# Last one-head attention and last mixture of a four-level network: products of weights and the first four tiles of rows made in the stage in front

## The chip, the cores and the metric

The kernel runs on one core of a Trainium2 chip: one program that computes the whole network in one launch. The metric is the device time of that launch in microseconds; three runs of the kernel before gave 1704.18, 1707.31 and 1710.19, median 1707.31 us.

## The reference

x has 32 batches of 32 tokens with 256 features (1024 tokens), context 32 x 257 x 192. Four levels follow each other, each with cross attention, self attention and a feed-forward part, and each part is `x = x + part(layernorm(x), ...)`. What matters here is the end of it:

```python
def L3_attn(x, Wq, bq, Wk, bk, Wv, bv, Wo, bo):        # one head, within each batch
    q, k, v = x @ Wq.T + bq, x @ Wk.T + bk, x @ Wv.T + bv
    qk = einsum('bsd,btd->bst', q, k)
    theta = 0.5 + 0.2 * sigmoid(qk) + 0.15 * tanh(qk) + 0.1 * relu(qk)
    out = einsum('bst,btd->bsd', softmax(theta), v)
    return out @ Wo.T + bo

def L3_ffn(x, Wg, bg, W1, b1, W2, b2):                  # mixture of 8 experts, best 2 of each token
    gates = softmax(x @ Wg + bg)
    g = gates on the two largest, divided by their sum
    return sum over e of g[e] * (gelu(x @ W1[e] + b1[e]) @ W2[e] + b2[e])

x = x + L2_ffn(layernorm(x), ...)                       # mixture with a capacity for each expert
x = x + L3_xattn(layernorm(x), ctx_768, ...)            # cross attention with the context
x = x + L3_attn(layernorm(x), ...)
x = x + L3_ffn(layernorm(x), ...)
```

## The kernel before

x lies in SBUF as 8 tiles of 128 tokens (four batches to a tile) by 256 features, beside xn (the normalised rows) and xnT (the same transposed, 2 chunks of 128 features by 1024 tokens). Each part of the network is a stage, a function of its own with one block in which the five engines have a list each; the lists are written out by hand, and semaphores order them against each other. At the end of a block all engines meet at a barrier, so a stage starts when the last of them is through, SP (which issues the DMAs) included.

The stages around the change, in order: `stage_scan`, `stage_moe_capacity` ("moecap" in tile names), `stage_xattn3` ("xattn"), `stage_attn3` (which calls `stage_one_head`, "attn"), `stage_moe` ("moe").

A stage that starts with a layernorm makes it in one of two ways. `Norm` (line 107) does all 8 tiles in the stage: statistics and moments on VectorE (L153, L156), the power -0.5 on GpSimd (L183, L186), rows on VectorE (L166), for attn3 some of them on ScalarE (L211), transposes on TensorE (L201), copies into xnT on ScalarE (L221), with `warm` (L61) giving TensorE idle matmuls to do during the statistics. `Ahead` splits it: rows 0 to 3 (tiles 0 to 3) are made in the end of the stage in front, rows 4 to 7 at the start of the own stage, beside matmuls on the first half. Its parts are `statistics`, `moments`, `power`, `rows`, `turn` and `take`, and its tiles and semaphores belong to the core. Six stages have it, among them the one-head attention of level 1 (`stage_attn1`), which shares the function `stage_one_head` with attn3; the branches `soft_theta` are attn3's.

**attn3 before.** SP issues eight loads of its weights and biases (L2098 to L2103), then `ew.sp`: two clearings of spare rows (L2994, L2995) and 16 loads of 1 MB, W1 and W2 of the eight experts of the last mixture (L3328, L3329, tile moe_w). The SBUF of these 16 MB is given out when `stage_xattn3` has ended, so they can't be loaded sooner. TensorE waits for its own eight loads, makes Wq.Wk ("QK", L2131), transposes xn, folds the biases (`fold_biases`, L2140 to L2148), makes Wv.Wo ("VO", L2131), then queries times QK (L2168), scores (L2182), values (L2193) and probabilities times values (L2201). VectorE adds each result to x (L2295).

**The mixture before.** `Norm` for all tiles, then `TopTwo`: logits by 32 matmuls (L2925) behind one wait for all four of its loads (L2908 to L2911, issued at the front of the stage by SP), choice of two experts on VectorE, ranks, then lists of rows for 23 blocks. Rows and gates are stored to DRAM (L3006 to L3009), GpSimd gathers each block's rows (L3415), TensorE does the two layers of each block (L3466, L3476), GpSimd adds the results into the output in DRAM. TensorE and VectorE wait for all of moe_w before the first block.

**The end of xattn3 before.** A pipeline over steps s = 0 to 12: scores(s), turned probabilities (s-1), probabilities times context (s-2, L3808), turned output (s-3, L3819), and for pairs of tiles values (L3830) and projection (L3840). In the last steps only the later pieces are left.

Of the kernel before, what the change touches and what calls it, by code (L numbers as in the profile page):

```python
# [6 lines left out]
ALU = mybir.AluOpType  # L7
ACT = mybir.ActivationFunctionType
F32 = mybir.dt.float32
# [6 lines left out]
P = 128  # L16
# [89 lines left out]
class Norm:  # L106
# [31 lines left out]
    def all_ready(self, eng, end=TILES):  # L138

        eng.wait_ge(self.xn_ready, len([t for t in self.by_dve if t < end]))  # L140
        if self.by_act:
            eng.wait_ge(self.xn_act_ready, len([t for t in self.by_act if t < end]))

# [1898 lines left out]
def stage_one_head(core, name, wq, wk, wv, wo, b_qkv, bo, ew=None, hw=None, ln=None, nx=None, lw=None):  # L2042
    nc, d = core.nc, core.dram
    soft_theta = hw is None
    with ExitStack() as ctx:
        st = Stage(core, ctx, name)
        if soft_theta:
            ln = Norm(st, shared=True)
            wq_s, wk_s, wv_s = [st.sb(n, [P, CD, D]) for n in ("wq", "wk", "wv")]
            qk = st.sb("qk", [P, CD, D])  # L2050
        else:
            wq_s, wk_s, wv_s, qk = hw.wq, hw.wk, hw.wv, hw.qk
        tT = st.sb("tT", [P, CD, TOKENS])
        v = core.xn if soft_theta else st.sb("v", [P, TILES, D])
# [6 lines left out]
        loaded = st.sem("loaded")  # L2061
        qk_done, qk_ready = st.sem("qk_done"), st.sem("qk_ready")
# [10 lines left out]
        if soft_theta:  # L2073
            wo_s, bo_s, b_s = st.sb("wo", [P, CD, D]), st.sb("bo", [P, D]), st.sb("b", [P, 3 * CD])
            bq_wide, bv_wide = st.sb("bq_wide", [P, CD, P]), st.sb("bv_wide", [P, CD, P])
            vo, key_b, query_b = st.sb("vo", [P, CD, D]), st.sb("key_b", [P, CD]), st.sb("query_b", [P, CD, SEQ])
            both_b, half_b, out_b = st.sb("both_b", [P, 1]), st.sb("half_b", [P, 1]), st.sb("out_b", [P, D])
            th_half, th_full = st.sb("th_half", [P, TILES * SEQ]), st.sb("th_full", [P, TILES * SEQ])
            relu, theta = st.sb("relu", [P, TILES * SEQ]), st.sb("theta", [P, TILES * SEQ])
            wide_ready, folded, fold_ready = st.sem("wide_ready"), st.sem("folded"), st.sem("fold_ready")  # L2080
            vo_done, vo_ready, out_b_ready = st.sem("vo_done"), st.sem("vo_ready"), st.sem("out_b_ready")
            relu_ready, tanh_ready, bo_added = st.sem("relu_ready"), st.sem("tanh_ready"), st.sem("bo_added")
            LOADS = 8
        else:
            vo = wv_s
# [3 lines left out]
        QK, VO, FOLD, OUT = bank[4], bank[5], bank[6][:, 0:2 * CD + 1], bank[6][:, D:2 * D]  # L2089
# [5 lines left out]
        def _(sp):  # L2095
            if soft_theta:
                for to, m in [(wq_s, wq), (wk_s, wk)]:
                    sp.dma_start(to[:, :, :], m.rearrange("(c p) n -> p c n", p=P)).then_inc(loaded, 16)  # L2098
                for n in range(3):
# [2036 lines left out]
```

## Time and profile before

| | before |
|---|---|
| median of 3 runs | 1707.31 us (1704.18 to 1710.19) |
| the profiled execution, its own time | 1711.28 us |
| its span | 1709.4 us |
| mean granted TensorE clock | 0.961 |
| TensorE busy | 1535.2 us, 90% of the span |
| VectorE, ScalarE, GpSimd busy | 1059.1, 837.4, 765.8 us |
| bytes moved by DMA | 204.51 MB, mean 120 GB/s |

Times in the profile are microseconds from the start of the span unless marked ns. PE is TensorE's matmuls, PEld its weight loads, DVE VectorE, ACT ScalarE, POOL GpSimd, SP the engine that issues most DMAs; SPq and POOLq are their queues' own instructions. `out<-in` names the tiles that an instruction writes and reads, `xN` counts instructions, and a bracket gives the engine's idle time in front and what ended it. In a timeline row the first number is the start, the second the time from there to the end of the last instruction of the row. PEclk 1.00 means 2.4 GHz and 0.50 means 1.2 GHz.

### The profile page before, as it was taken

The numbers are of one execution on the slowest core, as the hardware profiler recorded it, in microseconds if no ns is written. First come the engines' busy times: TensorE is split into PE (matmuls) and PEld (weight loads), VectorE is DVE, ScalarE is ACT, GpSimd is POOL, SyncE is SP. The second block draws the span as 40 slices with busy tenths as digits, with TensorE's granted clock in tenths as the row PEclk, the third lists the DMA queues.
The fourth block names the chain that finished last, engine by engine and source line by source line (L and its number), as shares of the span: only waits on it lengthen the run. The fifth ranks groups of instructions, "written<-read, shape, count | busy, mean of one in ns | idle before, by whom it ended". The sixth has DMA issues, their size and how long they took to land. (4 is left out here: it accounts for less than half of the span.)

```text
span 1709.4 us, 37142 instructions
## 1 busy us (share of the span) xinstructions
PE 1535.2 (90%) x13507; PEld 1315.5 (77%) x13507; DVE 1059.1 (62%) x2934; ACT 837.4 (49%) x2414; POOL 765.8 (45%) x894
## 2 busy tenths in 40 slices
PE   7999999988788999987999999998859788859998
PEld 6898898957567999975888988874539744649997
DVE  4888877645866888865866776748941132353332
ACT  4666666645335888851766666650013222213332
POOL 7666555442338999953311111226833311213332
PEclk9999999999999999999999999999979988879999
DMA  8554454312003333312633333425047272952221
GB/s 267 185 164 157 161 172 158 105 68 83 1 1 116 132 131 131 133 42 83 196 116 106 106 106 113 145 78 181 1 124 216 27 232 93 345 178 33 38 39 26
DMA packets 127221, 204.51 MB, mean 120 GB/s; under 512 B 21034, under 2 KB 92362, under 8 KB 126658
## 3 DMA queue, kind: packets, MB, share of 16 engines
q1 hardware_dynamic: 119016, 188.83, 34.2%
q0 software_dynamic: 6720, 8.79, 3.3%
q10 hardware_dynamic: 1306, 4.51, 0.8%
q8 instruction: 111, 1.82, 0.4%
q14 instruction: 68, 0.56, 0.1%
HBM read 161.76 MB, written 41.14 MB: 119 GB/s over the span
## 5 line engine op out<-in xcount | busy, mean ns | idle before, releaser
L1073 DVE TENSOR_SCALAR xattn_oT<-banks,xattn_last 128x256 f32<-128x256 f32 x254 | 110.9, 478 | 90.5 <-PE banks L854 90.1
L962 ACT ACTIVATE xattn_probs<-banks,xattn_negmax 128x257 f32<-128x257 f32 x256 | 123.9, 484 | 62.4 <-DVE xattn_negmax L1054 62.3
L967 ACT ACTIVATE xattn_probs<-xattn_probs,xattn_rsum 128x257 f32<-128x257 f32 x256 | 131.8, 515 | 1.4 <-DVE xattn_rsum L1058 1.4
L1350 POOL TENSOR_SCALAR xattn_probs<-xattn_probs,xattn_rsum 128x257 f32<-128x257 f32 x128 | 119.5, 934 | 23.2 <-DVE xattn_rsum L1622 23.1
L1054 DVE TENSOR_REDUCE xattn_negmax<-banks 128x1 f32<-128x257 f32 x256 | 106.4, 416 | 34.7 <-PE banks L820 33.1
L765 POOL COPY ctx_stat<-xattn_mv 128x2 f32<-128x2 f32 x32 | 6.0, 187 | 237.1 <-DVE xattn_mv L1087 237.1
L973 ACT CAST xattn_probsT_hi<-banks 128x256 fp32r<-128x256 f32 x256 | 95.5, 373 | 31.5 <-PE banks L829 27.6
L1063 DVE TENSOR_TENSOR xattn_probsT_lo<-banks,xattn_probsT_hi 128x256 fp32r<-128x256 f32 x256 | 105.0, 410 | 7.1 <-ACT xattn_probsT_hi L973 6.0
L829 PE MATMUL banks<-ident,xattn_probs 128*128 128x128 f32 x512 | 103.9, 285 | 3.6 <-ACT xattn_probs L967 3.2
L715 POOL TENSOR_SCALAR xattn_ctxT<-xattn_rawT 128x514 fp32r<-128x514 f32 x32 | 49.8, 1558 | 100.0 <-issue 94.7
L816 PE MATMUL banks<-xattn_ctxT,xattn_qk_hi 128*128 128x258 f32 x256 | 93.7, 366 | 0.5 <-DVE xattn_qk L1050 0.5
L3466 PE MATMUL banks<-moe_xinT,moe_w_now 128*128 128x128 f32 x736 | 88.3, 279 | 0.0
L3466 PEld LDWEIGHTS banks<-moe_xinT,moe_w_now 128*128 128x128 f32 x736 | 86.5, 196 | 0.1
L849 PE MATMUL banks<-xattn_probsT_hi,xattn_ctxN 128*128 128x256 f32 x256 | 85.0, 332 | 1.1 <-issue 1.1
L3424 POOL DMA_INDIRECT out_dram<-moe_y_slots,moe_row_u x23 | 36.4, 1584 | 110.2 <-DVE moe_y_slots L3591 107.2
L798 PE MATMUL banks<-xattn_qT,xattn_wk 64*128 64x128 f32 x1024 | 73.3, 283 | 11.9 <-DVE xattn_qT L1039 10.2
L3476 PE MATMUL banks<-moe_w,moe_hT 128*128 x368 | 83.1, 379 | 0.0
L2727 POOL TENSOR_TENSOR scan_product<-scan_state,scan_qT 128x1024 f32<-128x1024 f32 x32 | 70.0, 2187 | 20.5 <-DVE scan_state L2874 18.4
L798 PEld LDWEIGHTS banks<-xattn_qT,xattn_wk 64*128 64x128 f32 x1024 | 62.2, 187 | 20.9 <-issue 13.1
L3510 ACT ACTIVATE moe_hT<-banks,moe_b_now 128x128 f32<-128x128 f32 x184 | 52.6, 368 | 47.1 <-PE banks L3466 47.1
L871 PE MATMUL banks<-xattn_oT,xattn_wv 128*64 128x128 f32 x1024 | 69.1, 278 | 7.2 <-issue 6.0
L780 PE MATMUL banks<-xnT,xattn_wq 128*128 128x128 f32 x512 | 69.7, 283 | 6.1 <-ACT xnT L221 2.3
(516 smaller groups left out, 5087.1 us busy)
## 6 DMA issues: line engine op xcount, KB each, us to landing
xattn_ctxT<-ctx_partsT SPq DMA_DIRECT2D x64, 516.0 KB, 4.0
xattn_ctxN<-ctx_partsN SPq DMA_DIRECT2D x64, 384.0 KB, 4.1
ctx_partsT<-xattn_ctxT SPq DMA_DIRECT2D x32, 516.0 KB, 2.7
moe_w<-in_L_ffn_W SPq DMA_DIRECT2D x16, 1024.0 KB, 12.9
ctx_partsN<-xattn_ctxN SPq DMA_DIRECT2D x32, 384.0 KB, 3.6
moecap_w_early<-in_L_ffn_w SPq DMA_DIRECT2D x10, 1024.0 KB, 9.2
xattn_rawN<-in_ctx SPq DMA_DIRECT2D x32, 192.0 KB, 2.7
xattn_raw<-in_ctx SPq DMA_DIRECT2D x32, 192.0 KB, 5.1
```

The costliest lines, as they stand in the source:

```text
L798: mm = nc.tensor.matmul(bank[:, k * P:(k + 1) * P], wk_s[r, h // 2, g % 2 * P:(g % 2 + 1) * P], qT[r, h // 2, :], start=True, stop=True, t ...
L816: nc.tensor.matmul(out, unit(qk1[0]), part(0, 0), start=True, stop=False)
L829: mm = nc.tensor.transpose(TB[n % 2][:, c * P:(c + 1) * P], probs[:, n % RING, c * P:(c + 1) * P], core.ident[:, :])
L849: nc.tensor.matmul(front[:, 0:2 * P], first_hi(c), hi[:, c], start=(c == 0), stop=False)
L962: nc.scalar.activation(probs[:, n % RING, :], SB[n % 2][:, 0:KV], ACT.Exp, bias=negmax[:, n % RING:n % RING + 1], accum_out=psum[:, n % RI ...
L967: nc.scalar.mul(probs[:, n % RING, :], probs[:, n % RING, :], rsum[:, n % RING:n % RING + 1]).then_inc(norm_ready, 1)
L973: nc.scalar.copy(probsT[0][:, n // 2 % PAIRS, :, n % 2, :], TB[n % 2][:, 0:2 * P].rearrange("p (c n) -> p c n", c=2)).then_inc(probsT_hi_r ...
L1054: nc.vector.tensor_reduce(negmax[:, n % RING:n % RING + 1], SB[n % 2][:, 0:KV], AX.X, ALU.max, negate=True).then_inc(negmax_ready, 1)
L1063: nc.vector.tensor_tensor(lo, TB[n % 2][:, 0:2 * P].rearrange("p (c n) -> p c n", c=2), hi, ALU.subtract).then_inc(probsT_ready, 1)
L1073: nc.vector.tensor_scalar(oT[k][:, heads, b, :], by_head(out_banks(n)[k][:, k * 2 * P:(k + 1) * 2 * P]), last[:, k, j * PER_TILE + b:j * P ...
L1350: nc.gpsimd.tensor_scalar(probs[:, n % RING, :], probs[:, n % RING, :], rsum[:, n % RING:n % RING + 1], None, ALU.mult).then_inc(norm_read ...
L3466: mm = nc.tensor.matmul(H[n % 2][k][:, f * P:(f + 1) * P], w1_now[:, c, at:at + P], xinT[:, n % 2, c, :], start=(c == 0), stop=(c == CD - 1))
```

## The change

Four things are moved. (1) The weights and biases of attn3 get tiles of their own at the other end of SBUF (`SoftWeights`), loaded by SP in `stage_moe_capacity` behind the last expert's weights. (2) Their products and the folding of the biases are made in the last steps of `stage_xattn3`: folding at s = 8, QK at s = 9, VO at s = 10, in banks that are free by then; ScalarE and VectorE take them a step later; GpSimd widens two bias columns at the start of that stage. (3) attn3's layernorm becomes an `Ahead`: statistics of rows 0 to 3 on VectorE at s = 9, rows at s = 12, transposes on TensorE at s = 11, copies at the end. (4) The last mixture's layernorm becomes an `Ahead` too: rows 0 to 3 in the end of attn3, rows 4 to 7 in the mixture, whose TensorE list is now: gate matmuls of half 0, transposes of rows 4 to 7, gate matmuls of half 1. The idle matmuls of `warm` fall away in both stages. SP's list in attn3 holds only `ew.sp`. attn3's values go into a tile of their own instead of xn, since xn now holds the next stage's rows.

```diff
+class SoftWeights:
+    LOADS = 8
...
+    def sp(self, sp):
+        for to, m in zip((self.wq, self.wk, self.wv, self.wo), self.drams):
+            sp.dma_start(to[:, :, :], m.rearrange("(c p) n -> p c n", p=P)).then_inc(self.loaded, 16)
+        for n in range(3):
+            sp.dma_start(self.b[:, n * CD:(n + 1) * CD], self.b_drams[n]).then_inc(self.loaded, 16)
+        sp.dma_start(self.bo[:, :], self.bo_dram.partition_broadcast(P)).then_inc(self.loaded, 16)
...
+    def product(self, out, left, right):
+        for c in range(CD):
+            for k in range(CD):
+                mm = self.nc.tensor.matmul(out[:, c * D:(c + 1) * D], left[:, k, c * P:(c + 1) * P], right[:, k, :],
+                                           start=(k == 0), stop=(k == CD - 1))
+        return mm
...
@@ stage_one_head @@
         @block.sync
         def _(sp):
             if soft_theta:
-                for to, m in [(wq_s, wq), (wk_s, wk)]:
-                    sp.dma_start(to[:, :, :], m.rearrange("(c p) n -> p c n", p=P)).then_inc(loaded, 16)
...
                 ew.sp(sp)
...
-            if soft_theta:
-                ln.warm(pe, 7)
-                pe.wait_ge(loaded, 16 * LOADS)
-                product(QK, wq_s, wk_s).then_inc(qk_done, 1)
-                ln.pe(pe)
-                fold_biases()
-                product(VO, wv_s, wo_s).then_inc(vo_done, 1)
-                pe.wait_ge(qk_ready, 1)
+            pe.wait_ge(hw.qk_ready, 1)
             for n in range(2):
-                if soft_theta:
-                    pe.wait_ge(ln.xnT_ready, CD * (n + 1))
-                else:
-                    if n:
-                        ln.turn(pe, 1, LATE)
-                    ln.transposed(pe, n)
+                if n:
+                    ln.turn(pe, 1, LATE)
+                ln.transposed(pe, n)
...
-            if not soft_theta:
-                nx.turn(pe, 0, NEXT)
+            nx.turn(pe, 0, NEXT)
...
@@ stage_moe_capacity, SP @@
                 cw.load(sp, e)
+            hw.sp(sp)
             bring(sp, range(0, TILES, 2))
...
@@ stage_moe @@
         @block.tensor
         def _(pe):
-            ln.warm(pe, 7)
-            ln.pe(pe)
             for h in range(2):
-                pe.wait_ge(ln.xnT_ready, CD * (h + 1))
+                ln.transposed(pe, h)
                 gate.pe(pe, h)
+                if h == 0:
+                    ln.turn(pe, 1, LATE)
...
@@ stage_xattn3 @@
+    FOLD_AT, QUERIES_KEYS_AT, VALUES_OUT_AT, TURN_NEXT_AT = TILES, TILES + 1, TILES + 2, TILES + 3
...
+        FOLD, QUERIES_KEYS, VALUES_OUT, NEXT = SB[0], SB[1], TB, OB
...
+            hw.wide(pool)
...
+            nx.power(pool, 0)
...
+                if s == FOLD_AT:
+                    pe.wait_ge(scaled_ready, TILES - 1)
+                    hw.fold_biases(pe, FOLD)
+                elif s == QUERIES_KEYS_AT:
+                    pe.wait_ge(scaled_ready, TILES)
+                    hw.queries_keys(pe, QUERIES_KEYS)
+                elif s == VALUES_OUT_AT:
+                    pe.wait_ge(probsT_ready, 2 * TILES)
+                    hw.values_out(pe, VALUES_OUT)
+                elif s == TURN_NEXT_AT:
+                    pe.wait_ge(o_ready, TILES)
+                    nx.turn(pe, 0, NEXT)
...
+                if s == QUERIES_KEYS_AT + 1:
+                    hw.take_queries_keys(act, QUERIES_KEYS)
+                elif s == VALUES_OUT_AT + 1:
+                    hw.take_values_out(act, VALUES_OUT)
+            nx.take(act, 0, NEXT)
...
+                if s == TURN_NEXT_AT + 1:
+                    nx.rows(dve, 0)
...
+                if s == FOLD_AT + 1:
+                    hw.take_biases(dve, FOLD)
+                    dve.wait_ge(x_done, 2)
+                    for t in Norm.HALVES[0]:
+                        nx.statistics(dve, t)
+                    nx.moments(dve, 0)
```

## Rows read from the trace of the kernel before

**Rows 1.** The chain that ended last, in order of time: start, us, what.

```profile
1508.26 1.52 PE banks L201 x8
...
1509.78 3.49 PE banks L2925 x32
```

**Rows 2.** Timeline of SP's issues, attn3 to mixture.

```profile
1452.85 0.39 SPq L2098 DMA_DIRECT2D attn_wq<-in_L_attn_Wq  x1
...
1457.95 0.59 SPq L3328 DMA_DIRECT2D moe_w<-in_L_ffn_W  x1
...
1495.13 0.95 SPq L3329 DMA_DIRECT2D moe_w<-in_L_ffn_W  x1
1502.92 0.37 SPq L2908 DMA_DIRECT2D moe_gate_w<-in_L_ffn_Wg  x1
```

**Rows 3.** Busy times by stretch; last PEclk, DMA share, GB/s.

```profile
1435.40:1448.20 12.80, 9.82 (x77) 5.38 (x76) 2.03 (x6) 4.30 (x10) 0.00 (x0) 1.00 0.01 1
1448.20:1452.80 4.60, 3.64 (x8) 2.36 (x8) 0.69 (x1) 0.00 (x0) 0.00 (x0) 0.63 0.00 0
...
1473.00:1502.90 29.90, 25.35 (x321) 17.76 (x320) 11.46 (x24) 4.71 (x12) 4.04 (x6) 0.94 1.06 376
```

**Rows 4.** DMA issues, KB each, us to landing (single issues, in six stretches).

```profile
moe_w<-in_L_ffn_W SPq DMA_DIRECT2D x1, 1024.0 KB, 7.0
...
moe_w<-in_L_ffn_W SPq DMA_DIRECT2D x1, 1024.0 KB, 12.2
...
moe_gate_up_to<-in_up_to SPq DMA_DIRECT2D x1, 128.0 KB, 3.7
...
moe_gate_w<-in_L_ffn_Wg SPq DMA_DIRECT2D x1, 8.0 KB, 2.9
...
moecap_gate_w<-in_L_ffn_gate_w SPq DMA_DIRECT2D x1, 8.0 KB, 1.9
...
moecap_w_early<-in_L_ffn_w SPq DMA_DIRECT2D x2, 1024.0 KB, 6.2
```

**Rows 5.** Waits of SP in attn3: total, times, longest, in us.

```profile
SPq L2045 <- PEq L2045: 6.6, 1, 6.6
```

**Rows 6.** Timeline of TensorE in the end of xattn3.

```profile
1437.76 0.33 PE L3819 MATMUL banks<-ident,xattn_o_norm 128*128 128x128 f32 x1 [1.03 <-ACT xattn_o_norm L3897]
...
1443.07 1.89 PE L3840 MATMUL banks<-xattn_wo,xattn_aT 128*128 128x256 f32 x8
...
1448.21 3.64 PE L3840 MATMUL banks<-xattn_wo,xattn_aT 128*128 128x256 f32 x8 [0.93 <-ACT xattn_aT L3914]
```

**Rows 7.** Timeline of TensorE in attn3: a product, and a part of the folding.

```profile
1460.56 3.78 PE L2131 MATMUL banks<-attn_wk,attn_wq 128*128 128x256 f32 x8 [3.82 <-DMA attn_bo<-in_L_attn_bo]
...
1466.53 0.95 PE L2140 MATMUL banks<-attn_b,attn_wk 128*128 128x1 f32 x8
```

**Rows 8.** Timeline of SP's issues in the capacity mixture.

```profile
1306.62 0.51 SPq L3042 DMA_DIRECT2D moecap_w_early<-in_L_ffn_w  x1
1366.35 1.77 SPq L3099 DMA_DIRECT2D x<-moecap_sum  x4
```

**Rows 9.** Timeline of the level-1 one-head attention.

```profile
767.40 3.70 PE L2168 MATMUL banks<-xnT,attn_qk 128*128 128x512 f32 x8 [1.16 <-ACT xnT L276]
...
780.74 1.03 PE L2201 MATMUL banks<-attn_v,attn_probsT 128*128 128x256 f32 x4
...
791.09 0.38 SPq L451 DMA_DIRECT2D xattn_wq<-in_L_xattn_w_q  x1
```

**Rows 10.** Timeline of attn3: first scores, first probabilities times values.

```profile
1480.00 0.31 PE L2182 MATMUL banks<-xnT,attn_tT 128*32 128x32 f32 x4
...
1496.97 1.03 PE L2201 MATMUL banks<-xn,attn_probsT 128*128 128x256 f32 x4
```

**Rows 11.** Timeline of the mixture: first layer of blocks 0 and 1.

```profile
1532.28 6.05 PE L3466 MATMUL banks<-moe_xinT,moe_w_now 128*128 128x128 f32 x32
...
1538.39 3.74 PE L3466 MATMUL banks<-moe_xinT,moe_w_now 128*128 128x128 f32 x32
```

More of the change, by code:

```diff
@@ L2107, in _ @@
         def _(pool):
+            ln.power(pool, 1)
+            nc.gpsimd.memset(probsT[:, :, :], 0.0).then_inc(probsT_zero, 1)
+            ln.normalised(pool, 1)
             if soft_theta:
[L2109 to L2114 removed]
@@ L2123, in _ @@
                 nc.gpsimd.tensor_tensor(x_plus[:, :, :], core.x[:, :, :], core.xn[:, :, :], ALU.add).then_inc(x_plus_ready, 1)
-                nx.power(pool, 0)
+            nx.power(pool, 0)
         @block.tensor
         def _(pe):
-            def product(out, left, right):
-                for c in range(CD):
-                    for k in range(CD):
-                        mm = nc.tensor.matmul(out[:, c * D:(c + 1) * D], left[:, k, c * P:(c + 1) * P], right[:, k, :],
-                                              start=(k == 0), stop=(k == CD - 1))
-                return mm
@@ L2185, in _ @@
             if soft_theta:
-                pe.wait_ge(vo_ready, 1)
+                pe.wait_ge(hw.vo_ready, 1)
             else:
@@ L2296, in _ @@
                                                ALU.mult, ALU.add).then_inc(x_done, 1)
-                if t == 4 and not soft_theta:
+                if t == 4:
                     dve.wait_ge(x_done, 4)
@@ L2301, in _ @@
                     nx.moments(dve, 0)
-            if not soft_theta:
-                nx.rows(dve, 0)
+            nx.rows(dve, 0)
 def head_weights(core, ctx, outer):
@@ L3003, in store @@
         for h, half in enumerate(Norm.HALVES):
-            ln.all_ready(sp, half[-1] + 1)
+            ln.normalised(sp, h)
             rows = self.x[half[0] * P:(half[-1] + 1) * P, 0:D]
@@ L3404, in _ @@
         def _(pool):
-            ln.pool(pool)
+            ln.power(pool, 1)
             gate.pool(pool)
@@ L3492, in _ @@
         def _(act):
-            ln.act(act)
+            ln.take(act, 1, LATE)
             gate.act(act)
@@ L3520, in _ @@
         def _(dve):
-            ln.dve(dve)
+            for t in Norm.HALVES[1]:
+                ln.statistics(dve, t)
+            ln.moments(dve, 1)
+            ln.rows(dve, 1)
             step = Chain(dve, steps)
@@ L3743, in _ @@
                 moments(t)
+            nx.power(pool, 0)
         @block.tensor
```

182 lines of the change are left out of this document (89 added, 93 removed).

## The prediction

> **What bounds the kernel now.** I read the page first: TensorE is busy nearly everywhere, but the slices around the two last stages thin out. The chain of work that ended last [rows 1] reaches back only to the start of the last mixture: statistics of all eight tiles, VectorE's and GpSimd's part, transposes, then 32 gate matmuls ending at 1513.27. In front of it the chain stops at a stage barrier, so I cut the end of the span at the barriers by SP's first issue of each stage [rows 2]: last one-head attention ("attn3") from 1452.85, mixture from 1502.92. That makes 50.1 us for attn3, and 60.4 us from attn3's start to the end of the gate. Call attn3's start S before and S' after the change; everything behind the gate is common to both kernels, so the sum is: how much later is S', and how much less than 60.4 us lies between S' and the end of the gate.
>
> The view that decides is not a compute engine's. SP issues 16 loads of the experts' weights (moe_w, 1 MB each, 16.8 MB) inside attn3, because their SBUF is only free then. The DMA engines run them at 376 GB/s through the whole rest of the stage [rows 3]. The first is issued at 1457.95 and lands 7.0 us later, at 1464.95 (S+12.1); the last is issued at 1495.13 and lands 12.2 us later, at 1507.33 (S+54.5) [rows 2, 4]: 15 further MB in 42.4 us. SP is held in its issues by the full queue and is done at 1496.1; it then waits 6.6 us for the barrier at the end of attn3 [rows 5]. So two limits lie close behind the compute path: the stage can't end before SP has issued its last load, and the gate's own loads stand behind 16.8 MB on the same queue.
>
> **The change part by part.**
>
> *End of the cross attention ("xattn3"), price of the moved work on TensorE.* Now TensorE has three waits of about 1 us there: 1.03 us before each of the last two turns of the normalised output, 0.93 us before the last projection [rows 6]. Added: 20 one-column matmuls and 4 of 256 columns (bias folding), two products of 8 matmuls each, 8 transposes. Eight one-column matmuls take 0.95 us with the last one's tail, so 20 take about 2.2 [rows 7]; 8 matmuls of 256 columns take 1.89 at the full clock [rows 6], so 4 take 0.94 and a product 1.9; 8 transposes took 1.52 with short waits for their rows in it [rows 1], so 1.0 to 1.5. Folding 3.1 less the 1.03 wait that it covers is +2.1; queries-keys 1.9 - 1.03 = +0.9; values-out, in front of nothing that waits, +1.9; transposes 1.0 to 1.5 against 0.93 = +0.1 to +0.6. Together +5.1. The last projection now runs at the low clock, 3.64 us for 8 matmuls against 1.89, just after a wait [rows 3, 6]; with the waits filled it may stay at 2.4 GHz, which gives 1.75 back: +3.4. Were all added work at 1.2 GHz it would cost about double (a product took 3.78 us at that level [rows 7]): +11. I take +4.0, between the two near cases. VectorE's share (five bias copies, statistics, moments and rows of four tiles) falls in its waits for TensorE, which does 8 to 10 us of work between two things that it wants of VectorE; in its order the copies stand behind the sums that ScalarE needs. ScalarE's four copies stand behind what the chain needs of it, the last two beside the projection. GpSimd's two widenings come in a stage start where it waits for loads anyway; its power stands behind its last moments of the context. I price these at 0; their cover is TensorE's added work itself, and if VectorE were late with the rows TensorE would wait in front of its last projection, at most 2 us.
>
> *Loads moved on SP's queue.* The eight small loads (1.2 MB) go from the front of attn3 to the capacity mixture behind the last expert's load, after which SP issues nothing from 1307.1 to 1366.35, when it brings x back [rows 8]: eight issues and 3 us of transfers fit there, 0. In attn3 the first moe_w issue moves from S+5.1 to about S'+1.2, with only the two clearings ahead of it. Two 1 MB loads issued into an empty queue landed 6.2 us after issue in the middle [rows 4], so about 5 for the first and 7.5 for the second; the first lands at S'+6.5 to 8.5, I take 7.3 (S+12.1 before), and at the same 42.4 us for the rest the last lands at S'+49.7, 4.8 us sooner in the stage.
>
> *attn3's compute.* Products, biases and rows 0 to 3 leave the stage. Scores start now at 1480.00, that is S+27.2 [rows 10]. The one-head attention of level 1 already has the new form: its second block of queries starts at 767.40, 6.8 us into its stage (from 760.6), and takes 3.7, so scores could begin at S'+10.5 [rows 9]. From scores to the product with the probabilities attn3 takes 16.97 us (1480.00 to 1496.97 [rows 10]), and from there to the next stage the level-1 attention, which prepares rows 0 to 3 for its follower, takes 10.35 (780.74 to 791.09 [rows 9]). Sum 37.8 us instead of 50.1. SP's limit: the last issue stays 12.2 us before the last landing, so S'+37.5, done 0.9 later: S'+38.4. The two meet; attn3 shrinks by about 11.7 us, and the mixture begins near S'+38.4.
>
> *The mixture.* Preparing rows 0 to 3 earlier would let the gate start sooner by a few us, but its four loads are now issued 11 us before the stream of moe_w has landed. They used to be issued behind a nearly drained queue and landed in 2.9 (weights) to 3.7 us (the triangular constant, at 1508.0) [rows 4]; one matmul wait covers all four. Now they land with the stream's end or a little after it: S'+50.0, from 49 to 52. TensorE, idle since about S'+37, then does 16 gate matmuls, 8 transposes of rows 4 to 7 (which stand behind these in its order, so are held by the loads too), waits for ScalarE's copies, and does 16 more. After an idle of similar length the first 32 weight-bound matmuls of the experts take 6.05 us against 3.74 for the next 32 [rows 11], so I take the first gate half at the low level: 3.5 (double of half of 3.49 [rows 1]), 1.5 for the turn, 1.4 for the copies, 1.8 to 3.5 for the second half: 8.2 to 9.9, take 9.1; all at the full clock it would be 1.75 + 1.1 + 1.4 + 1.75 = 6.0. End of the gate: S'+59.1 against S+60.4: -1.3. The 18 us of VectorE and GpSimd work behind it don't change; stores of the rows land by about S'+60, and the gathers that need them come near S'+73.
> The Trainium skill, "TensorE: Matmul & The Clock Gate", section "What's actually happening", says that the throttled state is the default and activity lifts it. The trace agrees: the low level stands in 1448.2 to 1452.8 behind a wait and 1.00 in the busy stretch before [rows 3]. By the rule the gate costs 9.1; without it, 6.0, and the end would come 3.1 sooner.
>
> **The sum.** +4.0 - 1.3 = +2.7 us. Against the profiled execution (1711.3 us, span 1709.4) that is 1714.0; the median of the runs is 1707.3, 4.0 lower, and the prediction stands against it: **1710.0**. The 12 us taken from attn3 are mostly lost again: before the change the experts' load and the compute ended within a few us of each other, and only the compute is shortened. Bounds of the unknown costs: tail +3.4 to +11, stream end S'+49 to 52, gate 6.0 to 9.9. All three at their low end: 3.4 + (55.0 - 60.4) = -2.0; a bad case, half of the added work at the low level: 8 + (61.9 - 60.4) = +9.5.
>
> **The rivals.**
> *The gate's loads pass the stream* (the faster side). For: the gate's weights, issued at 1502.92, landed at 1505.8, 1.5 us before the last moe_w that was issued 7.8 us earlier [rows 2, 4]. Against: the same load took 1.9 us in the capacity mixture, where the queue was empty, so it did wait 1.0 us here. Price if they pass freely: the mixture starts at S'+38.4 and the loads land 5.1 us into it as now, the gate ends 11.5 us into it, S'+49.9; -10.5 + 4.0 = -6.5, so 1700.8. Chance 0.08.
> By the Trainium skill, "DMA: Bandwidth & Descriptors", section "Queues, rings and completion order", descriptors of one ring are taken up in order on each DMA engine though a later one may complete its write first. By that rule passing is limited to small amounts like the 1.5 us seen, and the rival dies; the trace agrees as far as it goes.
> *The tail of xattn3 at 1.2 GHz* (slower side). The clock there is uneven: 1.00 until 1448.2, then 0.63 [rows 3], though TensorE was mostly busy. If it falls as soon as the folding starts, the added work costs +11 and the other matmuls up to 2 us more: +13 - 1.3 = +11, 1718. It decides from about 2 us of added cost over my +4.0: then the total passes +5.1, a measurable loss. Chance, with milder forms, 0.24.
> *The clock holds and the stream starts promptly:* -2 to +1 us, 1705 to 1708, chance 0.25; it is the lower half of my case.
> *The move doesn't shorten attn3 at all*, because SP's issues stretch: then M moves, but the gate still hangs on the stream; no different time. It is inside the forecast.
>
> **How the numbers follow.** Forecast case (+1 to +5 us) 0.40, the clean case 0.25, passing loads 0.08, something of that sign that I don't see 0.03, slow tail 0.24. A measurement of this kernel tells about 0.3% (5.1 us) from no change. Faster by more: 0.11; within: 0.65; slower: 0.24. Range: from -6 (part of the passing case, and the spread of 3 us that the runs show) to +10: 1701.5 to 1717.5.
>
> **What would show it.** Right: attn3 about 38 us long with SP issuing until just before its end; the last moe_w landing near S'+50; TensorE waiting for a DMA of the gate's loads for 5 us or more in the mixture; xattn3's last stretch about 4 us longer, its three waits gone. Wrong: gate matmuls that start within 7 us of the mixture's start (passing loads), a granted clock of 0.5 through the tail of xattn3, or an attn3 that is longer than 45 us, which would put the statistics of rows 4 to 7 in front of the gate again.

## The result: 0.29% slower, and the profile after

The changed kernel takes 1716.06 us, median of 20 runs (1709.96 to 1722.84), against 1709.93 us (1703.97 to 1720.87, 20 runs) for the kernel before on the same chip: a ratio of 1.0029, 95% interval 1.0015 to 1.0043. In this kernel's time that is +5.0 us (+2.6 to +7.4); forecast were +2.7. (The ratio is not the quotient of the two medians, which would be 1.0036, or 6.1 us, inside the same interval.)

The profiled execution of after took 1713.57 us (span 1711.7, mean clock 0.958) against 1711.28 (1709.4, 0.961), a difference of only 2.3. That number hides something: xattn3 starts 4.3 us sooner in it (SP's first load of the context at 1367.63, before at 1371.97), in front of everything that bears on the time here; over all kernels below that start lies between 1367.6 and 1377.2. So I cut the end of each span at four points that all these kernels share: SP's first issue in xattn3, in attn3 and in the mixture, and GpSimd's first gather of rows. All lengths below are differences of two starts in the timelines of SP and GpSimd; the clock is TensorE's granted clock in the ten microseconds from 50 to 60 us into xattn3, "held" where it stayed at 1.00 in them and "fell" where it didn't; it says nothing of the rest of the stage.

| kernel | xattn3 | clock there | attn3 | mixture to first gather | attn3's start to first gather | rest of the span |
|---|---|---|---|---|---|---|
| before | 80.9 | 0.50 fell | 50.1 | 24.6 | 74.7 | 181.9 |
| after | 87.2 | 0.61 fell | 39.1 | 36.2 | 75.2 | 181.6 |
| e1 turn first | 84.5 | 0.64 fell | 38.9 | 33.0 | 71.8 | 181.8 |
| e2 gate's loads first | 80.0 | 1.00 held | 39.6 | 26.4 | 66.0 | 181.7 |
| e3 two experts late | 84.4 | 0.61 fell | 35.7 | 29.3 | 65.0 | 182.1 |
| e4 before, gate's loads first | 82.7 | 0.50 fell | 46.0 | 25.7 | 71.7 | 180.5 |
| e5 light tail | 78.7 | 0.61 fell | 39.7 | 36.0 | 75.7 | 181.0 |
| e6 norm left in the mixture | 84.2 | 0.61 fell | 39.1 | 33.0 | 72.0 | 181.9 |
| e7 idle matmuls in the gate's wait | 80.3 | 1.00 held | 39.2 | 33.4 | 72.7 | 181.8 |
| e8 = e2 + e5 | 83.7 | 0.63 fell | 41.2 | 26.3 | 67.5 | 180.9 |
| e9 before, filled | 77.6 | 1.00 held | 50.2 | 24.6 | 74.8 | 181.7 |
| e10 after, filled | 80.8 | 1.00 held | 39.9 | 36.0 | 76.0 | 181.4 |
| e11 = e2 + e3 + e5 | 78.8 | 0.61 fell | 39.0 | 27.1 | 66.1 | 181.9 |
| e12 = e11, filled | 77.7 | 1.00 held | 41.9 | 27.2 | 69.2 | 180.8 |

The last column is nearly constant, so what happens behind the first gather is common to all, as the prediction assumed. The first two rows hold the result. The 11.0 us that attn3 lost came back as 11.6 in the mixture, and xattn3 grew by 6.3. The chain that ended last used to start with the statistics of the mixture and lead through the transposes to the gate [rows 1]. In after it goes through SP and a load (start, us, what):

```profile
1493.88 3.82 SPq L2911
...
1499.48 6.08 DMA moe_gate_up_to<-in_up_to
...
1505.70 3.56 PE banks L2928 x16
1509.26 1.81 PE banks L272 x8
...
1511.10 1.08 ACT xnT L279 x2
...
1512.22 3.60 PE banks L2928 x16
```

SP's issues in after, the counterpart of [rows 2]: the first expert's load 1.2 us into attn3 (5.1 before), the last one until 1493.49, and then the gate's four loads. The issue of an 8 KB load alone holds SP for 3.82 us, where it held it for 0.37 before.

```profile
1454.82 0.53 SPq L2997 DMA_DIRECT2D moe_rows<-in_zeros  x1
1455.40 0.59 SPq L2998 DMA_DIRECT2D out_dram<-in_zeros  x1
1456.04 0.59 SPq L3332 DMA_DIRECT2D moe_w<-in_L_ffn_W  x1
...
1492.55 0.94 SPq L3333 DMA_DIRECT2D moe_w<-in_L_ffn_W  x1
1493.88 3.82 SPq L2911 DMA_DIRECT2D moe_gate_w<-in_L_ffn_Wg  x1
...
1499.48 0.43 SPq L2914 DMA_DIRECT2D moe_gate_up_to<-in_up_to  x1
```

What these loads took from issue to landing (KB, then us; four single issues in four stretches), the counterpart of [rows 4]: 9.6 us for the gate's weights and 6.1 for the triangular constant, where it was 2.9 and 3.7.

```profile
moe_w<-in_L_ffn_W SPq DMA_DIRECT2D x1, 1024.0 KB, 5.3
...
moe_w<-in_L_ffn_W SPq DMA_DIRECT2D x1, 1024.0 KB, 12.2
...
moe_gate_w<-in_L_ffn_Wg SPq DMA_DIRECT2D x1, 8.0 KB, 9.6
...
moe_gate_up_to<-in_up_to SPq DMA_DIRECT2D x1, 128.0 KB, 6.1
```

TensorE in the mixture of after, and its clock in the two stretches (in the second fence the columns are as in [rows 3]). It does nothing for 16.94 us, the last 11.8 of them in the mixture, waiting for the constant, and then runs all of the gate at 1.2 GHz.

```profile
1505.70 3.56 PE L2928 MATMUL banks<-moe_gate_w,xnT 128*128 128x8 f32 x16 [16.94 <-DMA moe_gate_up_to<-in_up_to]
1509.11 1.95 PE L272 MATMUL banks<-ident,xn 128*128 128x128 f32 x8
1512.22 3.58 PE L2928 MATMUL banks<-moe_gate_w,xnT 128*128 128x8 f32 x16 [1.16 <-ACT xnT L279]
```

```profile
1493.80:1505.60 11.80, 0.00 (x0) 0.00 (x0) 3.06 (x12) 0.00 (x0) 1.27 (x2) 0.50 1.03 314
1505.60:1516.00 10.40, 8.94 (x40) 8.47 (x40) 0.06 (x1) 1.07 (x2) 0.60 (x2) 0.50 0.96 294
```

The end of xattn3 in after, the counterpart of [rows 6]: the three waits are gone, the moved work stands in their place, and the last projection takes 1.99 us, not 3.64.

```profile
1436.45 1.65 PE L2102 MATMUL banks<-attn_wo,attn_bv_wide 128*128 128x256 f32 x4
...
1442.92 1.99 PE L2079 MATMUL banks<-attn_wk,attn_wq 128*128 128x256 f32 x8
...
1446.69 1.89 PE L2079 MATMUL banks<-attn_wo,attn_wv 128*128 128x256 f32 x8
...
1450.83 1.09 PE L272 MATMUL banks<-ident,xn 128*128 128x128 f32 x8
1451.83 1.99 PE L3850 MATMUL banks<-xattn_wo,xattn_aT 128*128 128x256 f32 x8
```

### The profile page after: what moved, and what is told of

Its sections match the earlier page's. It is cut to its first block and busy times, and to the rows that moved or that the text cites. A ratio compares the mean times of both kernels' runs of the same rounds, so it can differ in the third digit from the quotient of the medians.

```text
span 1711.7 us, 37082 instructions
## 1 busy us (share of the span) xinstructions
PE 1526.9 (89%) x13475; PEld 1310.2 (77%) x13475; DVE 1060.8 (62%) x2936; ACT 835.3 (49%) x2410; POOL 766.8 (45%) x894
## 5 line engine op out<-in xcount | busy, mean ns | idle before, releaser
L718 POOL TENSOR_SCALAR xattn_ctxT<-xattn_rawT 128x514 fp32r<-128x514 f32 x32 | 49.9, 1559 | 97.4 <-issue 92.4
L2730 POOL TENSOR_TENSOR scan_product<-scan_state,scan_qT 128x1024 f32<-128x1024 f32 x32 | 70.0, 2186 | 22.3 <-DVE scan_state L2877 20.4
L2877 DVE TENSOR_TENSOR_SCAN scan_state<-banks,scan_decay 128x528 f32<-128x528 f32 x64 | 75.0, 1241 | 1.5 <-PE banks L2759 1.5
L874 PE MATMUL banks<-xattn_oT,xattn_wv 128*64 128x128 f32 x1024 | 69.2, 278 | 7.2 <-issue 6.1
```

## The experiments

Theory: attn3 is now bound by SP's issue of the experts' loads, the gate by loads that stand behind them, and the work moved into xattn3 is paid there in full. The rival explanations for the loss are the tail of xattn3 alone (its price or its clock), and the split gate. Each ratio below is against the kernel before on the same chip (29 to 35 runs), with 12 runs of the edited kernel, 7 in e3 and 6 in e8.

### e2: the gate's loads ahead of the experts'

The four loads get tiles and a semaphore of their own and are issued in attn3 in front of `ew.sp`; `gate.sp` in the mixture falls away.

```diff
+        gl = GateLoads(core, ctx, ew.E, dram["L3_ffn_Wg"], dram["L3_ffn_bg"])
...
+                gl.sp(sp)
                 ew.sp(sp)
...
-            gate.sp(sp)
```

> The changed kernel with the gate's four loads issued by SP in attn3 in front of the experts' 16 loads, into tiles of their own. Theory: the mixture starts about 40 us after attn3's start and the gate ends 9 to 10 us into it, at 50 instead of 61: 11 us less, about 0.9965 of the kernel before; the other constants (b2, 1 MB) then land about when VectorE wants them, which can cost 0 to 2 us of this. Rival (the stream of 16.8 MB also bounds what comes behind the gate, through the stores of the rows): 0 to 3 us less. Rival (loads are not the bound): no change, 1.003.

Measured: 0.9971 (0.9957 to 0.9985). From attn3's start to the first gather it takes 66.0 us, 9.2 less than after. The first gate half starts 0.2 us after the mixture does:

```profile
1493.09 3.55 PE L2949 MATMUL banks<-early_gate_w,xnT 128*128 128x8 f32 x16 [5.61 <-PEq L2126]
1496.62 1.97 PE L272 MATMUL banks<-ident,xn 128*128 128x128 f32 x8
1499.76 3.58 PE L2949 MATMUL banks<-early_gate_w,xnT 128*128 128x8 f32 x16 [1.16 <-ACT xnT L279]
```

So the loads were what the gate waited for, and four small issues in another place turn the loss into a gain of 0.3%, somewhat less than expected. What is late next is the barrier: attn3 still takes 39.6 us (5.61 us of it TensorE's wait for the stage's end).

### e4: the same early loads in the kernel before

The same edit on the kernel before.

> The kernel before with the same early gate loads as in the run of that kind on the changed kernel. Theory (before the change the layernorm's chain reached the gate at 1509.6, 1.5 us after the last of its loads had landed, so the loads only became the bound by the change): no difference, 1.000, within 1 us. Rival (the loads or the stream already set the gate's time before): 1 to 5 us less.

Measured: 0.9986 (0.9968 to 1.0004), no difference that can be told. There the gate starts when its transposes and TensorE's earlier work are done, not when a load lands (it then takes 4.81 us and not 3.49, since the granted clock falls to 0.50 in its second half):

```profile
1506.48 1.41 PE L201 MATMUL banks<-ident,xn 128*128 128x128 f32 x8 [0.20 <-DVE xn L166]
1508.20 1.41 PE L201 MATMUL banks<-ident,xn 128*128 128x128 f32 x8 [0.32 <-DVE xn L166]
1509.44 4.81 PE L2946 MATMUL banks<-early_gate_w,xnT 128*128 128x8 f32 x32
```

The edit is worth about 10 us to the changed kernel (0.9971 against 1.0029 is 0.58%) and 0.14% or nothing to the one before: the exposure of these loads was made by the change. (In this run attn3 took 46.0 us, 4.1 less than in before, at a clock of 1.00 in its second twelve microseconds instead of 0.83; the ratio shows no gain of that size, so I take it for a difference of this one execution.)

### e3: two experts' loads left to the mixture

Experts 6 and 7 (four of the sixteen loads) are issued in the mixture behind its small loads.

```diff
-        for e in range(self.E):
+        for e in range(first, end):
...
+            ew.sp(sp, 6, E)
             rows.store(sp, ln, gate, stored, begun)
```

> The changed kernel with the loads of experts 6 and 7 (4 MB of 16) issued in the mixture, behind the gate's loads and constants, instead of in attn3. Theory (SP's held issues set the end of attn3, the stream the gate's start): attn3 ends with its compute, about 35.5 us after its start instead of 39; the gate's loads find 12 MB nearly landed and land at about 40, the gate ends at about 50 instead of 61: 11 us less, 0.9965 of the kernel before. Rival: the later end of the stream (about 54) or the stores behind it hold the first block, and 0 to 3 us are left.

Measured: 0.9958 (0.9941 to 0.9975). Attn3 takes 35.7 us instead of 39.1; it is then ended by arithmetic, and SP has been idle for 9 us (its last issue in attn3 ends 26.6 us into it):

```profile
1483.78 0.47 SPq L3334 DMA_DIRECT2D moe_w<-in_L_ffn_W  x1
1493.36 0.37 SPq L2911 DMA_DIRECT2D moe_gate_w<-in_L_ffn_Wg  x1
...
1499.69 3.25 SPq L3333 DMA_DIRECT2D moe_w<-in_L_ffn_W  x1
1502.98 1.12 SPq L3334 DMA_DIRECT2D moe_w<-in_L_ffn_W  x1
1504.14 6.30 SPq L3009 DMA_DIRECT2D moe_rows<-xn  x2
```

This shows the other limit: SP's issues end attn3 in after, 3.3 us behind where arithmetic ends it here. The cost is in the last line: the stores of the rows are now the ones that are held, and the first gather waits for the store of the gates behind them (`<-DMA moe_rows<-moe_gate_weight`), not for the list of rows.

### e1: all transposes ahead of the gate

```diff
+            ln.turn(pe, 1, LATE)
             for h in range(2):
                 ln.transposed(pe, h)
                 gate.pe(pe, h)
-                if h == 0:
-                    ln.turn(pe, 1, LATE)
```

> The changed kernel with one swap in the mixture's TensorE list: transposes of rows 4 to 7 in front of the first gate half instead of behind it. Theory (the gate waits for its own loads, which stand behind the stream of expert weights): in the changed kernel the wait ends 50.9 us after attn3's start and gate, transposes, copies and gate take 10.2 us from there. With the swap the transposes and copies are done during the wait, and only 32 matmuls at the low clock are left, 7.0 us: 3 us less, about 1.001 of the kernel before. Rival (the gate is bound by rows 4 to 7 or by the clock alone, not by loads): no change, 1.003.

Measured: 1.0010 (0.9988 to 1.0032). The transposes of rows 4 to 7 and their copies now lie in the wait for the constant, and the gate is one piece of 6.97 us where it was 10.1:

```profile
1501.73 1.97 PE L272 MATMUL banks<-ident,xn 128*128 128x128 f32 x8 [8.90 <-DVE xn L260]
1509.79 6.97 PE L2928 MATMUL banks<-moe_gate_w,xnT 128*128 128x8 f32 x32 [6.09 <-DMA moe_gate_up_to<-in_up_to]
```

The stretch to the first gather is 3.2 us shorter, as in the table. The ratio alone, 0.19% under that of after, doesn't prove it, since the intervals overlap.

### e6: the mixture's layernorm left whole in the mixture

Parts (1) to (3) of the change are kept, part (4) is undone: `Norm` with its idle matmuls in `stage_moe`, nothing of it in attn3.

```diff
-        stage_attn3(core, oh, to_attn3, to_moe, ew)
-        stage_moe(core, ew, to_moe)
+        stage_attn3(core, oh, to_attn3, None, ew)
+        stage_moe(core, ew)
```

> One part of the change alone: products, biases and rows 0 to 3 of attn3 as changed, but the mixture's layernorm whole in the mixture as before, with its idle matmuls. Theory: attn3 still ends with SP, about 39 us; the layernorm fits into the wait for the gate's loads, and behind these stand only the 32 gate matmuls: 7 us at the low clock instead of 10.2, so 3 us less than the whole change, about 1.001. That is, the rows prepared ahead for the mixture bring nothing and their place in TensorE's order costs 3 us. Rival (the ahead rows do bring their 2 to 4 us): 1.004 to 1.005.

Measured: 1.0001 (0.9979 to 1.0022). attn3 takes 39.1 us with or without the rows of the mixture in it (SP ends it), and the mixture reaches its first gather 3.2 us sooner:

```profile
1504.34 1.16 PE L204 MATMUL banks<-ident,xn 128*128 128x128 f32 x8
1505.76 1.41 PE L204 MATMUL banks<-ident,xn 128*128 128x128 f32 x8 [0.26 <-DVE xn L169]
1512.17 6.97 PE L2932 MATMUL banks<-moe_gate_w,xnT 128*128 128x8 f32 x32 [5.01 <-DMA moe_gate_up_to<-in_up_to]
```

Even the whole layernorm inside the mixture is 5.01 us ahead of the loads. Preparing half of the rows earlier brings nothing while they are late, and the order that comes with it (half a gate, transposes, the other half) puts 3.2 us of transposes and copies behind the wait. In this form part (4) is a loss, by the table; by the ratios it is likely (1.0001 against 1.0029, intervals that overlap).

### e7: idle matmuls in the gate's wait

```diff
                 ln.transposed(pe, h)
+                if h == 0:
+                    core.keep_busy(80, 7)
                 gate.pe(pe, h)
```

> The changed kernel with 80 idle matmuls (bf16, 256 columns) on TensorE in the mixture while it waits for the gate's loads. Theory: the gate, transposes, copies and gate take 6 to 6.5 us at the full clock instead of 10.2: 3.5 to 4 us less, about 1.0007 of the kernel before. The granted clock before the gate should read 1.00. Rival (these matmuls are bound by weight loads that don't follow the clock): no change, 1.003.

Measured: 1.0010 (0.9991 to 1.0029).

```profile
1489.69 10.96 PE L61 MATMUL banks<-ident 128*128 128x256 bf16 x80 [5.83 <-PEq L2126]
1501.21 1.95 PE L2928 MATMUL banks<-moe_gate_w,xnT 128*128 128x8 f32 x16 [0.57 <-DMA moe_gate_up_to<-in_up_to]
1503.02 1.07 PE L272 MATMUL banks<-ident,xn 128*128 128x128 f32 x8
1505.26 3.58 PE L2928 MATMUL banks<-moe_gate_w,xnT 128*128 128x8 f32 x16 [1.16 <-ACT xnT L279]
```

The first half takes 1.95 us, the transposes 1.07: full clock. The second half, behind a wait of 1.16 us, takes 3.58 again. So the gate came to 7.6 us, not to the 6.0 of a full clock: the idle matmuls bought 2.5 us of 4.1. The ratio doesn't separate this kernel from after. Its profiled execution is the fastest of its twelve runs (1706.73 against a median of 1713.01), and the table shows at least one reason: its clock held in the middle of xattn3.

### e5: only the QK product in the tail

The folding and the VO product go back into attn3, between its queries; QK, the statistics and the transposes stay in xattn3's end.

```diff
-                if s == FOLD_AT:
-                    pe.wait_ge(scaled_ready, TILES - 1)
-                    hw.fold_biases(pe, FOLD)
-                elif s == QUERIES_KEYS_AT:
+                if s == QUERIES_KEYS_AT:
...
+                if n and soft_theta:
+                    hw.values_out(pe, bank[5])
...
+                if n == 0 and soft_theta:
+                    hw.fold_biases(pe, bank[6])
```

> The changed kernel, but only the queries-keys product is made in the end of xattn3: folding of the biases and the values-out product go back to attn3 (weights still loaded early), behind the first block of queries and in front of the second. Theory: the tail of xattn3 gets about 4 us shorter, and the work lands in attn3 where compute ended 3.6 us before SP had issued its last load; the stream starts 4 us sooner, attn3 keeps its 39 us, perhaps 40, and the gate still waits for the stream: 3 to 4 us less than the change, about 1.0008 of the kernel before. Rival (the tail's price is hidden or lies elsewhere): no change, 1.003.

Measured: 0.9979 (0.9962 to 0.9995), more than expected. To price the tail apart from what the clock does in the middle of the stage I cut xattn3 once more, at the start of TensorE's probs_ctx(6), the last but one of its `xattn_N,xattn_probsT` rows; TensorE's list in front of this cut is the same in all kernels but for the idle matmuls of e9, e10 and e12.

| tail of xattn3 | from probs_ctx(6) to the end, us | granted clock in it |
|---|---|---|
| old: before, e9, e4 | 17.4, 17.5, 17.8 | 0.90, 0.90, 0.88 |
| whole, as in after: after, e1, e6, e3, e2, e7 | 22.3, 22.2, 22.0, 21.9, 21.9, 21.9 | 0.90 to 0.92 |
| whole, in e10 | 20.2 | 1.00 |
| only QK: e5, e11 | 16.7, 16.5 | 0.99, 1.00 |
| only QK: e12, e8 | 19.6, 21.6 | 0.83, 0.75 |

The ratio gained 0.50% on after, about 8.5 us, where the tail is 5.2 to 5.9 us shorter; the intervals leave room for the difference, and no run explains it.

So the folding and the VO product cost 5.2 to 5.9 us in the end of xattn3, or 3.6 to 3.8 where the clock stayed at full level with them (e10), and at most 0.6 in attn3, because SP ends that stage anyway. The difference between 22 and 20.2 is a fall of the clock inside the tail: in all six kernels of the second row the clock was back at 1.00 in the one-column matmuls of the folding and went down with the four wide ones behind them, also in e2 and e7, where it had held before. In e10 it stayed up. The wide matmuls, e6 first, e10 second:

```profile
1443.00 2.03 PE L2102 MATMUL banks<-attn_wo,attn_bv_wide 128*128 128x256 f32 x4
```

```profile
1433.04 1.11 PE L2102 MATMUL banks<-attn_wo,attn_bv_wide 128*128 128x256 f32 x4
```

QK, put in a wait with the transposes in the next one, costs less than nothing where the clock holds (16.5 and 16.7 against 17.4), since the last projection behind them takes 1.99 us and not 3.64. That is not assured: in e8 and e12 the clock fell in front of QK (3.78 and 3.37 us instead of 2.00), and the same tail took 21.6 and 19.6. The rows of e5:

```profile
1440.54 2.00 PE L2079 MATMUL banks<-attn_wk,attn_wq 128*128 128x256 f32 x8
1442.59 1.89 PE L3857 MATMUL banks<-xattn_wo,xattn_aT 128*128 128x256 f32 x8
...
1447.72 1.99 PE L3857 MATMUL banks<-xattn_wo,xattn_aT 128*128 128x256 f32 x8
```

### e8 and e11: the edits together

e8 is e2 with the light tail of e5; e11 adds the two late experts of e3.

> Early gate loads and light tail together. Theory: the gains add, since one lies before attn3's start and the other behind its end: 0.9971 - 0.0022, about 0.995 of the kernel before, if SP still sets attn3's end; where compute (now 3 to 4 us longer) sets it, about 1 us less of the gain. Rival: the constants of the mixture, which land with the stream's end, hold VectorE behind the gate, and nothing is added beyond 0.9965.

> Gate's loads issued ahead of the experts', only the QK product in the tail, and the loads of experts 6 and 7 left to the mixture: the three edits that each gained. In the run with the first two the stage of one-head attention took 41.2 us, of which SP's issue of the last expert's loads sets the end; without those two experts it took 35.7 us with the folding made ahead, and the folding and the VO product give back about 2.5 of it. Theory (each edit lifts a different limit, so they add): the mixture starts 2 to 3 us earlier than with two of them, first gather 1.3 us later, ratio 0.9925 against 0.9932. Rival (with the gate's loads early and the tail light, arithmetic ends last in the attention, and SP gave nothing): 0.994, since the late experts' loads only stand ahead of the stores.

Measured: e8 0.9932 (0.9905 to 0.9959, 6 runs), e11 0.9966 (0.9951 to 0.9981). e8 is faster than before and than after, and it is so although its profiled xattn3 took 83.7 us, at a clock of 0.67 and 0.68 in the twenty microseconds before its last 3.7. The interval of e8 (6 runs) barely meets those of e2 and e11. e11 brings no more; that much the rival had, but it came out above the rival's 0.994 too. Attn3 falls to 39.0 us, where arithmetic ends it (SP's last issue ends 29.4 us into it), 2.2 less than in e8, but the first gather comes 0.8 us later in the mixture and the rest of the span is 1.0 longer. In these profiles held experts pay only as long as SP ends attn3.

### e9, e10 and e12: the clock in xattn3

20 idle matmuls of 256 columns, ten each in front of two of TensorE's waits in the middle of xattn3, in the kernel before (e9), in the changed one (e10) and in e11 (e12).

```diff
+                if s == 7:
+                    pe.wait_ge(scaled_ready, 6)
+                    idle(10, SB[1])
                 if s < TILES:
...
+                if s == 7:
+                    pe.wait_ge(oT_ready, 8)
+                    idle(10, OT)
                 if 0 <= s - 3 < TILES:
                     turn_out(s - 3)
```

> The kernel before with 20 idle matmuls of 256 columns in the stage with the 768-wide context: ten ahead of the last block's scores, where TensorE waits 1.2 to 1.8 us for a load, ten ahead of the next turn of the outputs, where it waits 1.3 to 1.4 us for ScalarE. Seven profiled runs show the granted clock at 0.50 to 0.6 in the 10 us behind these two waits, two (both of kernels with the whole tail) show 1.00 there, and their stage took 80.0 and 80.3 us where three others of the same tail took 84.2, 84.4 and 84.5. Theory (the clock falls on these two waits, and work in them holds it): the stage takes about 77 us instead of 80.9, ratio 0.9978. Rival (the fall has another cause, or lies before them): no change of the stage, ratio 1.000 to 1.0006, since 20 matmuls of 0.11 us are 2.2 us of which most lies in the waits.

> The changed kernel with the same 20 idle matmuls. Theory: the tail then stands at full clock, the stage takes 80 us as in the two runs that kept the clock, and the ratio is 1.0004, against 1.0029 without; set against the run of the kernel before with the same idle matmuls, what is left is the price of the tail at full clock, by the sum 3.4 us or 0.2%, and the later gate. Rival (the fall has another cause): 1.003.

> The same with the 20 idle matmuls of the two fill runs. Theory (they hold the clock through the tail): 2 to 4 us less again, ratio 0.990 to 0.991. Rival: the same ratio as without them.

Measured: e9 0.9996 (0.9980 to 1.0012), e10 1.0017 (0.9997 to 1.0037), e12 0.9954 (0.9934 to 0.9974). The same ten microseconds of xattn3 in before, e9 and e10 (columns as in [rows 3], one row of each kernel in this order):

```profile
1421.97:1431.97 10.00, 9.53 (x48) 3.88 (x40) 2.69 (x10) 3.15 (x7) 0.79 (x5) 0.50 0.24 80
```

```profile
1422.91:1432.91 10.00, 9.10 (x76) 5.52 (x76) 3.15 (x11) 3.86 (x9) 1.99 (x7) 1.00 0.24 83
```

```profile
1419.01:1429.01 10.00, 8.70 (x75) 5.35 (x76) 3.15 (x11) 3.86 (x9) 2.34 (x8) 1.00 0.25 86
```

The clock held in this stretch in e9, e10 and e12, and xattn3 took 77.6 us in e9 and 80.8 in e10: 3.2 more, of which 2.8 lie in the tail (17.5 and 20.2 us). In e9 only the last projection ran at the low level (3.68 us, as in before), in e10 nothing in the tail did. That is the price of the tail at full clock. What the ratios say is weaker: e9 should have come to 0.9978 and came to 0.9996, so the 3.3 us that the profile shows are gained in part of the executions only, or lost elsewhere. The 1.0004 expected of e10 lies in its interval; e12, expected at 0.990 to 0.991, can't be told from e11, as its rival had it.

For e12 the profile shows one such place. Its xattn3 is 1.1 us shorter than that of e11, but attn3, in which TensorE's first 15 us are the same row for row, is 2.9 us longer. It doesn't begin with the clock: in the middle of the scores TensorE stands still for 2.97 us, waiting for nothing that the profile shows ("issue"), and only behind that the clock goes to 0.50. The same wait stands in the scores of before, e4, e9 and e10 (2.96, 3.03, 3.18 and 3.33 us); in the other nine it is 0.96 to 1.68 us and lies further on, in the values. Before first, then after, then e12:

```profile
1488.00 0.22 PE L2182 MATMUL banks<-xnT,attn_tT 128*32 128x32 f32 x1 [2.96 <-issue]
```

```profile
1474.46 0.92 PE L2213 MATMUL banks<-attn_vo,xnT 128*128 128x256 f32 x3 [1.40 <-issue]
```

```profile
1473.84 0.21 PE L2207 MATMUL banks<-attn_query_b,xnT 128*32 128x32 f32 x1 [2.97 <-issue]
```

So 20 matmuls added in one stage came with a later product with the probabilities in the next, by 3.1 us in both pairs (27.8 against 24.7 us into attn3 in e10 and after, 31.1 against 28.0 in e12 and e11). In e10 that is hidden behind SP, in e12 it is not. What TensorE waits for there stays open.

The Trainium skill, "TensorE: Matmul & The Clock Gate", section "HAM oscillation — how this bites in real kernels", says that a kernel whose matmul bursts are shorter than the waits between them can drop to the low level again and again. The trace agrees only in part. In after TensorE waits 1.80 us, works for 1.6, waits 1.33 and is at the low level behind that; but in before it worked from 1405.0 to 1419.3 without a wait in its rows, then waited once, for 1.50 us, and the scores behind that wait are at the low level already. Why the clock held in e2 and e7 behind 1.27 and 1.42 us, 1.19 and 1.42 us, and fell in e6 behind 0.98 and 1.31 us, stays open.

## Why the prediction was right

The forecast was +2.7 us, within 0.3%, range -6 to +10; measured +5.0 (+2.6 to +7.4), or 0.29%, just inside the 0.3% that it took for no change. Twenty runs of each kernel tell it from nothing. Both terms of the sum came out on the slow side, by 0.5 and 1.9 us. By its own steps:

- *The tail of xattn3*, +4.0 from bounds +3.4 and +5.1. From probs_ctx(6) to the end of the stage the profiles show 17.4 to 17.8 us in the kernels with the old tail and 21.9 to 22.3 with the whole new one, +4.9 in the pair before and after, and +4.5 between the medians of the two groups (17.5 and 22.0). (The whole stage is +6.3 in that pair, but of this 0.8 lie ahead of the fall of the clock that both have, and 0.6 in the last projection before the tail, 3.62 us against 3.02.) The size holds, and so does the argument that the last projection gets its full clock back. That it is so near is in part luck: at full clock the tail costs +2.8 (e9, e10), under the lower bound, and the rest, about 1.7, goes with stretches at the low level that the forecast case didn't have. What I had not seen is the granted clock of 0.50 just in front of the tail, in before as well: I read [rows 3] from 1435.40 on and took 1.00 for what the tail starts with. In the tail of after the clock went down a second time, in the wide matmuls of the folding (1.65 us for four; 1.11 in e10). The rival of a tail at 1.2 GHz was therefore nearer than its chance says. Its price was mis-added, too: by the prediction's rows the added work is 7.9 to 8.4 us, so twice that less the three waits is +13 to +14, and not +11.
- *The stream.* First landing foretold at 7.3 us into attn3, found 6.5 (1456.04 + 5.3); last landing foretold at 49.7, found 49.9 (1492.55 + 12.2).
- *attn3.* Foretold 38.4 us, with SP's issue and arithmetic meeting (37.8); found 39.1. The two don't meet: arithmetic alone ends it at 35.7 (e3), 2.1 less than my sum. The parts taken from the level-1 attention were right (10.5 us to the scores, found 10.47; 10.35 for the last part, found 10.8). The one that is off is the middle, which I took from attn3 itself: 16.97 us from the scores to the product with the probabilities, found 14.24 in after and 14.43 in e3. The 16.97 hold the wait of 2.96 us shown above, which in after is 1.40; the prediction didn't take that stretch apart. Since SP ended the stage, this cost the forecast nothing.
- *The gate's loads.* Foretold 50.0 us into attn3 (49 to 52), found 50.7 (1505.56). The rival that they pass the stream is dead (its price was too low as well: it gave the gate 6.4 us behind its loads, against the 9.1 of the forecast case): the 8 KB took 9.6 us and landed 1.3 us before the last expert's load (1503.5 against 1504.8), as in before, where it was 1.5; the constant landed 0.8 behind it. The rule that the prediction took from the Trainium skill, "DMA: Bandwidth & Descriptors", section "Queues, rings and completion order" (one ring is taken up in order, a later piece may end its write first), agrees with that.
- *The gate.* Foretold 9.1 us, found 10.1. The mis-sized term is the second half: I left open whether it would be back at full clock (1.8 to 3.5) and took the middle; it stayed low behind the 1.16 us wait for ScalarE (3.58), in after and even in e7 where the first half ran at full level.
- *The sum.* VectorE's first instruction on the gate starts 61.1 us behind attn3's start (1515.94), in before 60.5 (1513.39): +0.6, not -1.3. First gather +0.6 (75.2 against 74.7). With +2.8 to +4.9 for the tail that makes +3.4 to +5.5, and the runs show +5.0. The last gate matmul ends 61.0 us behind attn3's start, 1.9 later than foretold: 0.7 are the loads', 1.0 the gate's own, the rest lies between their rows.

Its main claim, that two limits stand close behind the arithmetic of attn3 and that the gain would end in them, is what e2 and e3 show, each by lifting one.

## What to carry to other kernels

Before work is moved out of a stage, read which limit ends that stage without it: here SP's issue of 16 MB of loads, and small loads that the next stage issues behind them, stood a few us behind the arithmetic, so 12 us of arithmetic bought nothing until four small loads had been moved ahead of the stream (1.0029 to 0.9971). Move only what fills waits: a product in a wait of 1 us cost nothing where the clock held, the folding and the second product cost xattn3 3.6 to 5.9 us, and 0.6 at most where they had been, since SP ended that stage. A stage that can't start on its own half-ready input should not be split: with the loads late, the half gate, transposes, half gate order was 3.2 us slower than the plain one.

## What was unexpected of the hardware

- An issue on SP's queue is not free while the experts' loads are under way: in attn3 of after every second 1 MB load held SP for 3.9 to 6.1 us from the fifth on, and the 8 KB load behind them held it for 3.82 and landed after 9.6. In e8 the first small load of the mixture held SP for 5.75 us.
- TensorE's granted clock falls and holds from one kernel to the next in the same code. Of eleven kernels without idle matmuls in xattn3 two held 1.00 from 50 to 60 us into the stage, nine fell to 0.50 to 0.64. From the last block's scores to probs_ctx(6), in all fourteen kernels, it took 10.0 to 10.6 us where the clock held and 14.0 to 15.2 where it fell. The tail behind that has falls of its own: the same list of instructions took 16.7 us in e5 and 21.6 in e8. That is as much as the change itself. A single profiled execution can't price an edit in that stage; the cut at fixed points and several kernels with the same tail could.
- TensorE stood still for 3.0 to 3.3 us in the middle of a list of small matmuls, waiting for nothing that the profile shows, in five of fourteen kernels, and for 1.0 to 1.7 us a little further on in the other nine. In both pairs of kernels that differ by idle matmuls in the stage in front of it, the filled one had the long wait and the other the short one.
